# A pipelined image kernel on one core: the norm-to-scan chain moved into the last four units, and three units a direction summed by VectorE

## The chip, the core and the metric

The kernel runs on one core of one Trainium2 chip. A core has five engines that run their own instruction streams side by side: TensorE (PE, matrix products into PSUM), VectorE (DVE), ScalarE (ACT), GpSimd (POOL) and SyncE (SP, which here only issues DMAs). Each stream runs strictly in its written order; between the streams stand semaphores, so an instruction that waits holds up all that is written behind it on its engine. The metric is the time of one launch in microseconds (us).

## The reference, cut to what matters

For 16 images of 256 channels by 32 x 32 pixels, two residual blocks:

```python
x = x + L0(_gn(x))     # attention over pixels makes a 7x7 filter per image and channel; depthwise convolution
x = x + L1(_gn(x))     # selective scans at three resolutions, both directions, gated by silu(z)

def _ssm(x, ...):      # one scan: 128 channels, 16 states, L = 1024, 256 or 64 positions
    delta = softplus(dts @ dtw + dtb);  dA = exp(delta * A);  dBx = delta * B * x
    h = h * dA + dBx   # over the L positions, for each of 16 states
    y = sum over the 16 states of h * C,  + x * Dv;  then a layer norm over the channels
y3 = ssm(f3) + flipped ssm(f3);  y2 = the same of f2 + up2(y3);  y1 = the same of f1 + up2(y2)
out = conv1x1(y1 * silu(z))
```

f1 is a 1x1 projection of the normed image, f2 and f3 come from it by 2 x 2 convolutions of stride 2.

## The kernel before, in words

**Pipeline.** `stages` writes for each engine a loop over images. Its body works on three images at once: i is in its scans (L1), j in its depthwise convolution and then in its norm, projections and first chunks (the beginning of L1), m in the making of its filters (the beginning of L0). The body has 37 units, k = 0 to 36, and then a `bridge` that ends image i and starts the scans of j. So in the next body j is i. Bodies with all three images run 14 times; one before and two after the loop, and one at the very start, lack some.

**Units.** `UNITS` lists the scans: unit 0 is the third level (64 positions, 16 states at once, both directions), units 1 to 4 the second level (256 positions, 4 states each, both directions), units 5 to 20 the first level forward (1024 positions, one state each), units 21 to 36 the first level backward. A product q is one unit and one direction. For a first-level unit k:
- SP reads the rows B and C of that state, spread over all partitions, into `bb` (two buffers) and `cb` (three buffers) (`get_b`, `get_c`).
- POOL multiplies `bb` by `u` into `bx` (`inputs`, line 1315), one unit ahead.
- ACT makes the decays exp(delta*A) in PSUM, `slot_b`, one half of 512 positions at a time (`decay`, line 1173).
- DVE scans each half into PSUM, `slot_c` (`scan`, line 552), and multiplies it by C into SBUF, `h` (`weigh`, line 561). The second half of a unit is weighed within the next unit.
- POOL adds `h` to the running sum `y` (`gather`, line 1343), one unit behind. `h` has three buffers.

**The image in the convolution.** PE does the 7 x 7 depthwise filter as 98 taps of six matmuls each (`taps`, line 790) with diagonal matrices that ACT makes (`make_row`, line 1059, 14 a row of the filter, in portions `row_parts` of 3 and 4). The last taps are in unit 32. `BRIDGE_TAPS` says how many taps of the next image are put into the last units and the bridge, and `ROOM` spreads the rest over the units (`taps_at`). PREP is unit 33.

**The last four units and the bridge.** DVE adds the convolution to the image (`conv_add(j, 1)`, line 486) and takes its statistics (`b_s0`, line 431) at the end of unit 33. PE and ACT turn them into mean and root in units 34 and 35 (`sums1`, `sums2`, `gn_spread`, `b1`), ACT writes the normed image `xg` (line 1105) in unit 35, PE projects it to f1 in unit 36 (`project_f`), and ACT copies f1 (`copy_f(j, 0)`, line 1112) in unit 36. In the bridge follow f2 and f3 (`lower`), then the chunks 0 and 1, which make delta and the rows B, C of the third and second level: `chunk` on PE (lines 831, 832), `chunk_exp` on ACT (lines 1124 to 1133), `chunk_first` on DVE (line 500), `chunk_log` on ACT (1139), `chunk_last` on DVE (508, 510), `chunk_low` on POOL (1285, 1287). Between them stand the last two norms of image i (`norm_centre`, `norm_square`, `norm_spread`, `norm_root`, `norm`), its `output` into `ob`, and at the end on DVE `silu_clip` and the two scans of the third level (`scan_least`, line 525). On ACT the bridge ends with the decays of unit 1 (they wait for `output`, which shares PSUM with them), `y_start`, `keep_x`, 21 diagonals and `copy_x`; chunk 2 comes right behind, in unit 0. For the image m, ACT writes the padded fp16 copy (`prep`, line 1048) in unit 33 and DVE its lower half (`low_half`, line 444) in unit 34.

## Time and profile before

| | |
|---|---|
| median of 3 runs | 4224.79 us (4222.85 to 4224.82) |
| the profiled execution, its time | 4222.54 us |
| its span, first to last instruction | 4220.7 us |
| POOL busy | 3290.3 us (78%) |
| DVE busy | 3209.0 us (76%) |
| PE busy, weight loads beside it | 3109.9 us (74%), 1400.2 us (33%) |
| ACT busy | 2693.2 us (64%) |
| DMA engines, mean busy share | 46.4% |

How to read it: no engine is busy for more than four fifths of the span, so the time is made of stretches with different limits. One body of the loop, about 250 us, is repeated with hardly a difference, and is read below in one instance, from 1202.6 to 1454.2 us of the span. In the rows an idle time in brackets is that of the engine just before the instruction, with what ended it.

### The profile page before, as it was taken

The page shows a single profiled execution, that of the slowest core. Times are in us where ns is not written, and L with a number is a line of the kernel's source. Part 1 is how long each engine was busy: PE and PEld are TensorE (multiplying, and loading weights), DVE is VectorE, ACT ScalarE, POOL GpSimd, SP SyncE. Part 2 cuts the span into 40 slices and gives each one's busy share as a digit, 9 for nine tenths or more (in the row PEclk, how much of TensorE's full clock was granted, in tenths as well). Part 3 has the DMA queues.
Part 4 walks back from the last instruction along what each step waited for, and adds up shares of the span by engine and source line. Part 5 has one row for each costly group of instructions (what it writes and reads, how often), then busy time and mean ns, then how long its engine had stood idle before and what let it go on. Part 6 is the DMA issues. An engine that isn't in the chain of part 4 may idle for free.

```text
span 4220.7 us, 53011 instructions
## 1 busy us (share of the span) xinstructions
PE 3109.9 (74%) x12620; PEld 1400.2 (33%) x12620; DVE 3209.0 (76%) x3975; ACT 2693.2 (64%) x6662; POOL 3290.3 (78%) x1908
## 2 busy tenths in 40 slices
PE   6978777887777788777777877788787778877511
PEld 3433333333333333333333433333333333333200
DVE  1058788787877878787887878788787887878877
ACT  4467766666766666666656766665677666666532
POOL 0059698796968969697896969889696987969797
PEclk8989888998888899889898988999898889988755
DMA  1025455453545545354553544445354554635544
GB/s 41 1 101 195 147 163 169 157 205 127 186 150 166 186 136 204 134 178 152 170 201 122 199 149 165 161 168 203 119 195 145 167 170 157 204 118 192 163 165 167
DMA packets 187275, 664.08 MB, mean 157 GB/s; under 512 B 22736, under 2 KB 24672, under 8 KB 186976
## 3 DMA queue, kind: packets, MB, share of 16 engines
q1 hardware_dynamic: 186976, 661.47, 46.4%
q14 instruction: 280, 2.29, 0.2%
q8 instruction: 19, 0.31, 0.0%
HBM read 639.76 MB, written 21.63 MB: 157 GB/s over the span
## 4 chain that ended last, share of the span: by engine, by line
POOL 28%; issue 19%; ACT 16%; PE 14%; DVE 13%; DMA 7%; POOLq 1%; DVEq 1%; SPq 0%; ACTq 0%
POOL bx L1315 13%; POOL y L1343 7%; DMA bb<-bc_rows 7%; ACT diag L1059 7%; PE pconv L790 6%; POOL h L1338 5%; DVE h L561 4%; DVE slot_c L552 2%; POOL bx L1318 2%; DVE rs L508 2%; ACT slot_b L1173 2%; PE pm L832 1%; PE pm L807 1%; PE pm L831 1%; DVE rs L500 1%
## 5 line engine op out<-in xcount | busy, mean ns | idle before, releaser
L790 PE MATMUL pconv<-pad,diag 128*128 128x512 f16 x9408 | 2270.5, 398 | 314.3 <-ACT diag L1059 210.0
L790 PEld LDWEIGHTS pconv<-pad,diag 128*128 128x128 f16 x9408 | 932.0, 100 | 1618.0 <-issue 346.0
L1343 POOL TENSOR_TENSOR y<-y,h 128x1024 f32<-128x1024 f32 (+2 forms) x672 | 1324.5, 1971 | 162.9 <-DVE h L561 139.6
L1173 ACT ACTIVATE slot_b<-delta,nega 128x512 f32<-128x512 f32 (+1 forms) x1280 | 805.4, 639 | 951.3 <-DVE slot_c L552 911.6
L1315 POOL TENSOR_TENSOR bx<-bb,u 128x1024 f32<-128x1024 f32 x512 | 1220.1, 2383 | 31.9 <-DMA bb<-bc_rows 31.9
L552 DVE TENSOR_TENSOR_SCAN slot_c<-slot_b,bx 128x512 f32<-128x512 f32 (+1 forms) x1024 | 954.4, 956 | 315.6 <-POOL bx L1315 214.6
L561 DVE TENSOR_TENSOR h<-slot_c,cb 128x512 f32<-128x512 f32 x1280 | 860.6, 674 | 35.9 <-POOL y L1343 35.9
L552 DVE TENSOR_TENSOR_SCAN slot_c<-slot_b,slot_c,bx 128x512 f32<-128x512 f32 x512 | 663.6, 1296 | 74.5 <-ACT slot_b L1173 18.2
L1059 ACT ACTIVATE diag<-id,chi 128x128 f16<-128x128 f16 x1568 | 498.1, 387 | 10.3 <-PE pconv L790 9.6
L1059 ACT ACTIVATE diag<-id,clo 128x128 f16<-128x128 f16 x1568 | 496.4, 386 | 0.0
L1338 POOL TENSOR_TENSOR h<-h 128x512 f32<-128x512 f32 (+3 forms) x384 | 349.9, 911 | 20.9 <-DVE h L531 3.4
L1285 POOL TENSOR_TENSOR delta<-delta,rs 128x512 f32<-128x512 f32 (+1 forms) x96 | 97.7, 1017 | 324.6 <-DVE rs L510 324.6
L1318 POOL TENSOR_TENSOR bx<-bb,u 128x1024 f32<-128x1024 f32 x64 | 158.8, 2482 | 125.5 <-DMA bb<-bc_rows 97.9
L500 DVE SCALAR_TENSOR_TENSOR rs<-qs,es 128x512 f32<-128x512 f32 (+1 forms) x96 | 64.9, 676 | 223.6 <-ACT qs L1133 223.6
L831 PE MATMUL pm<-f,wbc 128*32 128x512 f32 (+1 forms) x192 | 102.3, 620 | 147.0 <-ACT delta L1129 74.2
L1295 POOL TENSOR_TENSOR f<-f,lnw 128x98 f32<-128x98 f32 x16 | 6.2, 388 | 182.8 <-ACT f L1003 182.8
L1139 ACT ACTIVATE qs<-qs 128x512 f32<-128x512 f32 (+1 forms) x96 | 50.5, 526 | 153.7 <-DVE rs L500 153.7
L852 PE MATMUL pm<-es,ones 128*128 128x512 f32 (+1 forms) x128 | 62.7, 573 | 113.2 <-ACT es L1183 113.2
L846 PE MATMUL pm<-y,cen 128*128 128x512 f32 (+1 forms) x128 | 60.3, 554 | 89.2 <-POOL y L1343 40.6
L722 PE MATMUL pm<-ident,xh 128*128 128x128 f32 x256 | 47.0, 343 | 98.3 <-ACT xg L1094 72.1
L832 PE MATMUL pm<-f,wdelta 128*128 128x512 f32 (+1 forms) x192 | 116.9, 698 | 0.0
L695 PE MATMUL pconv<-sg,grp 128*128 128x8 f32 x32 | 9.5, 371 | 145.5 <-DVE sg L431 145.5
(171 smaller groups left out, 3095.9 us busy)
## 6 DMA issues: line engine op xcount, KB each, us to landing
bb<-bc_rows SPq DMA_DIRECT2D x592, 512.0 KB, 4.4
cb<-bc_rows SPq DMA_DIRECT2D x592, 512.0 KB, 4.4
xr<-in_x SPq DMA_DIRECT2D x16, 1024.0 KB, 5.0
out<-ob SPq DMA_DIRECT2D x16, 1024.0 KB
bc_rows<-rows SPq DMA_DIRECT2D x64, 64.0 KB, 1.6
w<-in_w SPq DMA_DIRECT2D x2, 256.0 KB
wc<-in_wc SPq DMA_DIRECT2D x2, 256.0 KB
bc_rows<-rows SPq DMA_DIRECT2D x16, 32.0 KB, 4.0
```

The costliest lines, as they stand in the source:

```text
L500: nc.vector.scalar_tensor_tensor(er[:, k, 0:n], qs[:, k, 0:n], 1.0, es[:, k, 0:n], ALU.subtract, ALU.subtract).then_inc(ch_err.sem, 1)
L552: ins = nc.vector.tensor_tensor_scan(hv, av, bv, start, ALU.mult, ALU.add)
L561: nc.vector.tensor_tensor(half(h[:, q % HR], b), bank(slot_c, b), half(cb[:, k % CR], b), ALU.mult).then_inc(q_pr.sem, 1)
L790: ins = nc.tensor.matmul(bank(pconv, k), w, pad[:, t, part, rows:rows + 16, dx:dx + W], start=first and m == 0, stop=last and m == 2)
L831: nc.tensor.matmul(bank(pm, 0)[0:2 * NS, 0:n], wbc[:, st, :], f[:, fc:fc + n], start=True, stop=True).then_inc(ch_bc.sem, 1)
L832: nc.tensor.matmul(bank(pm, 1)[:, 0:n], wdelta[:, st, :], f[:, fc:fc + n], start=True, stop=True).then_inc(ch_dt.sem, 1)
L1059: ins = nc.scalar.activation(diag[:, r % RING, m, dx, :], id16[:, :], ACT.Copy, scale=(chi, clo)[m][:, t, dy * KK + dx:dy * KK + dx + 1])
L1173: ins = nc.scalar.activation(slot_b[:, o:o + w], delta[:, so + c:so + c + w], ACT.Exp, scale=nega[:, st, n0 + n:n0 + n + 1])
L1315: ins = pool.tensor_tensor(bx[:, k % 2, :], bb[:, k % BR, :], us, ALU.mult)
L1318: ins = pool.tensor_tensor(o, bb[:, k % BR, :].rearrange("p (m l) -> p m l", m=m), us[:, None, :].to_broadcast([P, m, ln]), ALU.mult)
L1338: pool.tensor_tensor(src[:, 0:m], src[:, 0:m], src[:, m:2 * m], ALU.add).then_inc(n_y.sem, 1)
L1343: pool.tensor_tensor(yv, yv, src[:, 0] if len(src.shape) == 3 else src, ALU.add).then_inc(q_y.sem, 1)
```

## The change

Two things are changed together.

**The chain moves.** In DVE's stream `conv_add(j, 1)` and `b_s0(j)` go from the end of unit 33 to its start. The sums on PE go from unit 34 to 33, `project_f` from 36 to 34, `lower` from the bridge to 35, `chunk(j, 0)` from the bridge to 36. In ACT's stream the spread, the root and the normed image go into unit 33, `copy_f` 0 and 1 into 35, `copy_f` 2, `chunk_exp(j, 0)` and `chunk_log(j, 0)` into 36, and `prep(m)` from the end of unit 33 to the end of unit 34. On DVE `chunk_first(j, 0)` stands ahead of the products of unit 36 and `chunk_last(j, 0)` behind them. In the bridge the first `scan_least` comes ahead of `norm(i, 4)` and the second behind `norm(i, 5)`; the 16 decays of the third level come ahead of `norm_square(i, 4)`. On PE unit 36 is `chunk(j, 0)` and three taps, and the bridge is `chunk(j, 1)`, one tap, `norm_centre` 4 and 5, one tap, `norm_spread` 4 and 5, two taps, `project_z`, `output`, three taps. SP issues `get_b(j, 0)` before it waits for the last products. `BRIDGE_TAPS` puts 11 taps ahead of unit 0 where there were 9.

**VectorE sums three units a direction.** `OWN` names the states 3, 8 and 13 of the first level: units 8, 13 and 18 forward, 24, 29 and 34 backward. POOL's `gather` leaves them out. DVE writes the first of each direction (units 8 and 24) straight from PSUM into `ob`, which is free then; for the others it multiplies within PSUM (`slot_c`) and then adds to `ob`, two instructions a half for one. The four norms of the first level add `ob` by a second matmul of 512 columns with `cen` (`norm_centre`).

```diff
+OWN = (3, 8, 13)
+def own(q):
+    u, _ = PRODUCTS[q]
+    return UNITS[u][0] == 1 and UNITS[u][3] in OWN
...
             def weigh(i, q, p):
...
+                if own(q):
+                    part, total = bank(slot_c, b), half(ob[:, PRODUCTS[q][1]], b)
+                    if UNITS[k][3] == OWN[0]:
+                        if p == 0:
+                            dve.wait_ge(ob_free.sem, ob_free.at(i + 1, 0))
+                        nc.vector.tensor_tensor(total, part, half(cb[:, k % CR], b), ALU.mult).then_inc(q_pr.sem, 1)
+                        return
+                    dve.wait_ge(q_h.sem, q_h.at(i, half_at(q, 1) + 1))
+                    nc.vector.tensor_tensor(part, part, half(cb[:, k % CR], b), ALU.mult).then_inc(q_own.sem, 1)
+                    dve.wait_ge(q_own.sem, q_own.at(i, 2 * kept(q) + p + 1))
+                    nc.vector.tensor_tensor(total, part, total, ALU.add).then_inc(q_pr.sem, 1)
+                    return
...
 @@ VectorE, bridge @@
                 if j is not None:
-                    chunk_first(j, 0)
-                if j is not None:
-                    chunk_last(j, 0)
+                    chunk_first(j, 1)
+                    scan_least(j, 0)
                 if i is not None:
                     norm(i, 4)
                 if j is not None:
-                    chunk_first(j, 1)
+                    chunk_last(j, 1)
                 if i is not None:
                     norm(i, 5)
                 if j is not None:
-                    chunk_last(j, 1)
+                    scan_least(j, 1)
                 if i is not None:
                     output(i, 0)
                     output(i, 1)
                 if j is not None:
                     silu_clip(j)
-                    scan_least(j, 0)
-                    scan_least(j, 1)
...
 @@ VectorE, unit @@
+                if j is not None and k == PREP:
+                    conv_add(j, 1)
+                    b_s0(j)
+                if j is not None and k == NU - 1:
+                    chunk_first(j, 0)
                 if i is not None:
                     products(i, k)
...
-                if k == PREP:
-                    if j is not None:
-                        conv_add(j, 1)
-                        b_s0(j)
                 if k == PREP + 1:
                     if m is not None:
                         low_half(m)
+                if j is not None and k == NU - 1:
+                    chunk_last(j, 0)
...
 @@ TensorE, norm_centre @@
+                last = max(v for v in range(NP) if own(v) and PRODUCTS[v][1] == d)
+                pe.wait_ge(q_pr.sem, q_pr.at(i, weighed(last)))
+                nc.tensor.matmul(o, cen[:, :], src, start=True, stop=False)
+                nc.tensor.matmul(o, cen[:, :], ob[:, d, c0:c0 + n], start=False, stop=True).then_inc(n_yc.sem, 1)
...
 @@ ScalarE, unit @@
+                if j is not None and k == PREP:
+                    row_parts(j, m, k, 0)
+                    act_b.start(act, j)
+                    gn_spread(act_b, j, sg, pconv, b_sums, b_spread)
+                if i is not None:
+                    if 1 <= k < NU - 1:
+                        decay(i, k + 1, 0)
+                if j is not None and k == PREP:
+                    b_root(j)
+                else:
+                    row_parts(j, m, k, 0)
+                if j is not None and k == PREP + 2:
+                    copy_f(j, 0)
                 if i is not None:
                     if 1 <= k < NU - 1:
                         decay(i, k + 1, 1)
+                if j is not None and k == PREP:
+                    b_normal(j)
+                if j is not None and k == PREP + 2:
+                    copy_f(j, 1)
                 if j is not None and k == PREP + 3:
-                    copy_f(j, 0)
+                    copy_f(j, 2)
+                    chunk_exp(j, 0)
                 row_parts(j, m, k, 1)
+                if j is not None and k == PREP + 3:
+                    chunk_log(j, 0)
...
-                    if k == PREP:
+                    if k == PREP + 1:
                         prep(m)
...
 @@ TensorE, unit @@
-                if m is not None and k == PREP + 2:
-                    taps(m, 0, BRIDGE_TAPS[1])
...
+                if j is not None and k == PREP + 1:
...
+                    project_f(j, 0)
+                    project_f(j, 1)
+                if k == PREP + 2:
+                    if j is not None:
+                        lower(j, 0)
+                    if m is not None:
+                        taps(m, 0, BRIDGE_TAPS[1])
+                    if j is not None:
+                        lower(j, 1)
                 if k == PREP + 3:
                     if j is not None:
...
+                        chunk(j, 0)
                     if m is not None:
                         taps(m, BRIDGE_TAPS[1], BRIDGE_TAPS[2])
...
-BRIDGE_TAPS = (0, 1, 3, 3, 3, 3, 6, 9)
+BRIDGE_TAPS = (0, 1, 4, 5, 6, 8, 11)
```

## Rows read from the trace of the kernel before

**Rows 1.** Stretch, length; busy PE, PEld, DVE, ACT, POOL (count); PE clock, DMA, GB/s

```profile
1202.60:1264.40 61.80, 42.20 (x136) 18.92 (x135) 42.69 (x49) 47.91 (x131) 29.09 (x16) 0.81 0.31 108
...
1277.10:1392.60 115.50, 87.92 (x350) 36.77 (x348) 95.75 (x121) 73.22 (x175) 106.88 (x65) 0.87 0.52 169
1392.60:1454.20 61.60, 56.19 (x281) 28.71 (x281) 52.46 (x65) 34.82 (x84) 61.52 (x31) 1.00 0.65 219
```

**Rows 2.** Waits between 1392.6 and 1454.2 us: total, times, longest, in us

```profile
DVE slot_c L552 <- POOL bx L1315: 4.5, 7, 0.8
...
PE pm L745 <- ACT f L1007: 2.2, 1, 2.2
```

**Rows 3.** Single lines over the span: count, duration in ns as min/median/max

```profile
L1343 POOL TENSOR_TENSOR y<-y,h x672: 317/2352/2815, 271.0 to 4197.7; 128x1024 f32<-128x1024 f32 x128, 128x256 f32<-128x256 f32 x32, 128x64 f32<-128x64 f32 x8
L444 DVE TENSOR_TENSOR pad<-xh,pad x32: 1223/1678/3366, 66.7 to 3711.8; 128x1024 f16<-128x1024 f32 x32
L561 DVE TENSOR_TENSOR h<-slot_c,cb x1280: 664/673/693, 270.4 to 4196.9; 128x512 f32<-128x512 f32 x183
```

**Rows 4.** Group by line: two operands, one in PSUM (busy us, mean ns | idle)

```profile
L619 DVE TENSOR_TENSOR o<-slot_b,sz 128x512 f32<-128x512 f32 x16 | 11.1, 692 | 0.6
```

**Rows 5.** Timeline of DVE, units 33 to 36 (start us, us, instruction, idle before)

```profile
1202.57 1.23 DVE L552 TENSOR_TENSOR_SCAN slot_c<-slot_b,bx 128x512 f32<-128x512 f32 x1
...
1206.30 0.69 DVE L603 TENSOR_TENSOR pm<-pm,rs 128x512 f32<-128x512 f32 x1
...
1208.77 1.28 DVE L486 SCALAR_TENSOR_TENSOR xn<-pconv,csc,xn 128x1024 f32<-128x1024 f32 x1
1210.09 2.47 DVE L431 BATCH_NORM_STATS2 sg<-xn 128x6 f32<-128x512 f32 x4
...
1216.19 4.96 DVE L444 TENSOR_TENSOR pad<-xh,pad 128x1024 f16<-128x1024 f32 x2
...
1229.96 1.27 DVE L561 TENSOR_TENSOR h<-slot_c,cb 128x512 f32<-128x512 f32 x2
```

**Rows 6.** Timeline of ACT, units 33 to 36 and chunk 0

```profile
1213.69 2.02 ACT L1048 ACTIVATE pad<-xh 128x1024 f16<-128x1024 f32 x2
...
1217.03 0.97 ACT L1059 ACTIVATE diag<-id,clo 128x128 f16<-128x128 f16 x3
...
1221.73 0.15 ACT L969 ACTIVATE sg<-pconv 128x4 f32<-128x4 f32 x1
...
1223.23 2.37 ACT L1105 ACTIVATE xg<-xn,sg 128x1024 f32<-128x1024 f32 x2
1225.51 0.67 ACT L1173 ACTIVATE slot_b<-delta,nega 128x512 f32<-128x512 f32 x1
...
1238.27 0.21 ACT L1124 ACTIVATE rows<-pm 32x64 f32<-32x64 f32 x1 [0.39 <-PE pm L831]
```

**Rows 7.** Timeline of DVE in the bridge and unit 1

```profile
1239.62 0.23 DVE L500 SCALAR_TENSOR_TENSOR rs<-qs,es 128x64 f32<-128x64 f32 x1 [8.39 <-ACT qs L1133]
...
1246.11 0.70 DVE L603 TENSOR_TENSOR slot_b<-slot_b,delta 128x512 f32<-128x512 f32 x1 [4.49 <-ACT delta L1196]
...
1255.02 1.61 DVE L628 SCALAR_TENSOR_TENSOR ob<-slot_c,vec,xc 128x512 f32<-128x512 f32 x2
...
1257.74 4.53 DVE L525 TENSOR_TENSOR_SCAN h<-a,b 128x1040 f32<-128x1040 f32 x2
```

**Rows 8.** Timeline of ACT, end of the bridge and chunk 2

```profile
1256.66 1.67 ACT L1173 ACTIVATE slot_b<-delta,nega 128x256 f32<-128x256 f32 x4 [2.73 <-DVE ob L628]
...
1271.18 0.57 ACT L1124 ACTIVATE rows<-pm 32x512 f32<-32x512 f32 x1
```

**Rows 9.** Timeline of PE: a centre matmul, the last taps, the bridge

```profile
1194.63 1.12 PE L846 MATMUL pm<-y,cen 128*128 128x512 f32 x2 [1.34 <-DVE o L588]
...
1200.36 2.83 PE L790 MATMUL pconv<-pad,diag 128*128 128x512 f16 x12
...
1238.43 1.89 PE L846 MATMUL slot_b<-y,cen 128*128 128x512 f32 x2
```

More of the change, by code:

```diff
@@ L87, in weighed, with added, kept @@
     return q + 1 if q < 2 else 2 * q
+OWN = (3, 8, 13)
+def own(q):
+    u, _ = PRODUCTS[q]
+    return UNITS[u][0] == 1 and UNITS[u][3] in OWN
+def added(q):
+    return sum(not own(v) for v in range(q))
+def kept(q):
+    return sum(own(v) and UNITS[PRODUCTS[v][0]][3] != OWN[0] for v in range(q))
 NHALF = 2 * (NP - 2)
@@ L863, in some @@
                         taps(m, BRIDGE_TAPS[lo], BRIDGE_TAPS[hi])
+                if j is not None:
+                    chunk(j, 1)
                 some(2, 3)
-                if j is not None:
-                    lower(j, 0)
-                some(3, 4)
-                if j is not None:
-                    lower(j, 1)
-                some(4, 5)
-                if j is not None:
-                    chunk(j, 0)
                 if i is not None:
@@ L875, in bridge @@
                     norm_centre(i, 5)
-                if j is not None:
-                    chunk(j, 1)
+                some(3, 4)
                 if i is not None:
@@ L880, in bridge @@
                     norm_spread(i, 5)
-                some(5, 6)
+                some(4, 5)
                 if j is not None:
@@ L1237, in unit @@
             def unit(i, j, m, k):
-                if j is not None and k == PREP + 1:
-                    act_b.start(act, j)
-                    gn_spread(act_b, j, sg, pconv, b_sums, b_spread)
-                if j is not None and k == PREP + 2:
-                    b1(j)
                 if i is not None:
```

56 lines of the change are left out of this document (25 added, 31 removed).

## The prediction

> **What bounds the kernel now.** I first read the busy time by stretches of one body, here 251.6 us long (1202.6 to 1454.2 us). From 1392.6 to 1454.2 us, the last first-level units ahead of unit 33, POOL is busy for 61.52 of 61.60 us: it sets the pace, and DVE idles for 61.60 - 52.46 = 9.1 us, half of it in waits for POOL's `bx` (4.5 us in 7 waits) [rows 1, 2]. PE is close behind: 56.19 us at the full clock. Here a product taken from POOL is worth something. From 1202.6 to 1264.4 us, units 33 to 36 and the bridge, it is the other way round: POOL is busy for 29.1 of 61.8 us, DVE for 42.7, ACT for 47.9, PE for 42.2 [rows 1]. Nothing is full, so this stretch is a chain over several engines. The timelines show it: on ACT diagonals stand between the links, unit by unit [rows 6]; DVE is idle for 8.39 us before `chunk_first(j, 0)` and 4.49 us before `norm(i, 4)` [rows 7]; and ACT, once `output` is done, works without a stop from 1256.66 to chunk 2 at 1271.18 us [rows 8]. Chunk 2 starts the next image's units, so what comes late at `output` comes late everywhere behind.
>
> **Part 1, the sums on VectorE.** POOL loses six additions of 2.35 us an image [rows 3]. DVE pays nothing for units 8 and 24 (one product a half, into `ob` and not `h`). For units 13, 18, 29 and 34 a half costs two instructions with one operand in PSUM, 0.69 us each [rows 4], for one of 0.67 [rows 3]: +0.71 a half, +1.4 a unit, 5.7 an image. A product within PSUM isn't in these rows; I take the nearest one. Its bounds: 0 more, or twice 0.69 a half if reading and writing PSUM don't overlap (+1.4 a unit again). What it brings depends on the place:
> - Units 18, 24 and 29 lie in or at the stretch that POOL bounds. It needs 3 x 2.35 = 7.05 us less there. DVE can give up its 9.1 us of idle time less 2 x 1.4, but part of that is the pipeline between instructions. PE has 61.6 - 56.2 = 5.4 us to give, less two further centre matmuls of 1.1 us each [rows 9], plus one tap less (6 of the 12 matmuls in 2.83 us, 1.4 us) [rows 9]: 4.6 us. I take -3.5 us a body; bounds 0 and -6.
> - Unit 8's saved time meets units in which DVE has no idle time, and unit 13 ends at chunk 4, which waits for `norm(i, 1)` on DVE. I take 0 and +0.7 us.
> - Unit 34 lies in the chain, below.
>
> **Part 2, the chain in the last units.** I lay the new streams out from the start of unit 33 on DVE, 1202.57 us, as zero, with the durations of before.
> - `conv_add` now stands first. The last taps end at 1203.19 [rows 9], 0.6, and norm 3's second centre matmul, ahead of them on PE, adds 1.1. So DVE waits until 1.7; 1.28 and 2.47 us [rows 5] bring the statistics to 5.5 (before: 1212.56, 10.0). The start is 4.5 us earlier, as meant.
> - DVE then does unit 33, 3.7 us (1202.57 to 1206.30), norm 3 with 2.4 (1206.30 to 1208.77) and unit 34, 3.7 and half of unit 34's extra, 0.7: it is done at 16.1.
> - ACT: sums, spread and their PE steps bring it to 8.1, root 1.5 (1221.73 to 1223.23), decay 0.6, `xg` 2.4 [rows 6], four diagonals 1.2: 13.8. Unit 34 has 14 diagonals and two decays; before, 1217.03 to 1221.73 held 14 and one, 4.7 us, so 5.3: 19.1. Only now comes `prep`, 2.0 us [rows 6]: 20.1 for its first half, 21.1 for the second.
> - `low_half` on DVE waits for it: **4 us of idle time that wasn't there**. Behind it on DVE are queued units 35 and 36, and for them wait POOL and ACT's decays. It runs while POOL has nothing to do, so its halves take 1.22 us, the minimum, and not 4.96 together [rows 3, 5]: done at 22.6.
> - ACT's `copy_f(j, 0)` stands behind the decay of unit 36, which needs unit 35's first scan, at 23.8. Before, from that decay (1225.51) to the end of `chunk_exp(j, 0)` (DVE goes on at 1239.62) it took 14.1 us with 28 diagonals [rows 6, 7]; now 20 stand there (-2.3) and the waits for `lower` are about as long: 12.1. So `chunk_exp(j, 0)` is done at 36.0. **The chain has moved by four units of program and by 1 us of time** (before 37.05).
> - But `chunk_first(j, 0)` now stands ahead of unit 36 on DVE, and DVE is done with unit 35 at 27.0 (22.6 + 3.7 + 0.7). It waits for **9 us**. Queued behind it: unit 36's scans and products, so POOL's last two sums, both centre matmuls, norms 4 and 5, `output`. Unit 36 takes 4.4 us (until 40.6) where it was done at 28.7 (1229.96 + 1.27).
> - From there: POOL's last sum until 43.0; two centres of four matmuls, 4.4 us at the rate of 1194.63, 7.2 at that of 1238.43 [rows 9], I take 4.4: 47.5; one tap and two spreads 51.0; root; norm 4 from 51.3, 2.2 us; `chunk_last(j, 1)` 0.9; norm 5 2.1: 56.4. `scan_least(j, 1)` has two SBUF operands and meets POOL's `bx` of unit 1: 2.3 us [rows 7] after a wait of 1.8: 60.5. `output` 3.2 us [rows 7]: 63.7. Before it ended at 1256.63, 54.1. So `output` comes **9.6 us later**; ACT's unbroken work from there to chunk 2 is the same [rows 8].
> - The two taps that leave units 0 to 32 for the bridge lie there beside waits; SP's earlier `get_b(j, 0)` ends nothing late.
>
> What I take for the shared path: the shortest `low_half` is 1.22 us, the longest 3.37 [rows 3]. The Trainium skill says in "SBUF — State Buffer", section "SBUF: two separate sides", that DVE with two SBUF inputs and GpSimd lock the shared port pair against each other for a whole instruction. By that rule the sums moved to DVE cost no lock, since one operand is in PSUM, and the trace agrees: 1280 products take 664 to 693 ns whatever POOL does [rows 3]. Without it `low_half` would end 2.5 us later and the scan 1.8 us earlier.
>
> **The sum.** A body: 9.6 + 0.7 - 3.5 = +6.8 us; 14 bodies, +95. The transition without m has no diagonals in the chain, so the waits are shorter: +3. The first pass, which has no scans to wait for but `prep` in the chain: +2. The last image alone: up to six sums of POOL less, against DVE's 5.7 and colder centres: -4. Together +96 on 4222.5, the profiled execution (which lies 2.3 below the median of 4224.8): 4319, on the median's scale **4321 us**.
>
> **The rivals.**
> 1. Slower by more: the centres and the taps at the lower clock (+2.8 a body), no gain in POOL's stretch (+3.5 against my sum). For it: the clock of the stretch is 0.81 already [rows 1], and PE will idle more. +12 a body, 4395 us.
> 2. Slower by less: POOL's relief in full (-6), the scan not held up (-1.8). +2.5 a body, 4260 us.
> 3. **Faster.** One mechanism: chunk 0's `qs` reaches DVE when it is done with unit 35. It decides at 27.0 in my count, 9 us ahead of 36.0; then `output` comes 0.6 us later and not 9.6, a body is 0.6 + 0.7 - 3.5 = -2.2, and the last image's 4 us less come on top: about 4190. For it: the 8.39 us that DVE idles there now [rows 7] would be filled by unit 36. Against it: ACT's order. The diagonals, the decay of unit 36 and `prep` stand ahead of `copy_f`, and ACT is busy for nearly all of it [rows 6].
> 4. No change: the wait is about 3 us long, and both parts cancel: +0 to +0.5 a body.
>
> **How the numbers follow.** Forecast 0.52, rival 1 0.16, rival 2 0.14, rival 3 0.13, rival 4 0.05. The range reaches from below rival 2 to a little above rival 1, 4245 to 4405; rivals 3 and 4 are left out, 0.18. 0.2% is 8.4 us, about what a measurement of this kernel can tell from no change. Faster 0.13, same 0.05, slower 0.82.
>
> **What would show it.** In the timeline of DVE: a wait of some 4 us before L444, of some 9 us before the first L500 with two units' products behind it, and none or little before norm 4. ACT's pads after 14 diagonals. The body longer by some 7 us, with POOL's busy time lower by 14 us and its idle time higher by 21. Between the middle of the backward units and unit 33 the pace of POOL's stretch a few us shorter. I am wrong if L500 for chunk 0 starts without a wait, if `output` ends less than 5 us later against unit 33's start, or if POOL's stretch shrinks by 7 us or more.

## The result, and the profile after

| kernel | median of the runs, us | profiled span, us | PE clock |
|---|---|---|---|
| before | 4223.8 (4221.4 to 4224.8) | 4220.7 | 0.873 |
| after | 4438.5 (4432.6 to 4441.0) | 4435.1 | 0.854 |

The ratio is 1.051, 95% interval 1.049 to 1.053: **slower, by 215 us**, where +96 was forecast and 4405 us was the range's upper end. Every time below is a median of runs in the chip's fast state; the one profiled run of e8 was in the slow state (7468 us), so e8 has a time and no stages.

Where the time went can be read off one event an image, the end of the last `output` step on VectorE (before L628, after L661). The first stands at 506.0 us before and at 530.3 us after (+24.3). Thirteen bodies follow, +183.8 (14.1 each, forecast 6.8), then the transition without m, +11.5 (forecast 3), and the last image, -5.2 (forecast -4). So most of the miss lies in the bodies, the rest in the first pass and the transition.

The means over the thirteen bodies, by stage, in us. A stage begins and ends at the start of a named instruction, `output` at its end; "late units" are first-level units 18 to 32:

| stage | before | after | change | forecast |
|---|---|---|---|---|
| `output` to chunk 2 | 17.6 | 17.6 | 0 | 0 |
| to unit 7 | 44.7 | 44.7 | 0 | 0 |
| unit 7 to unit 10 | 17.0 | 19.9 | **+2.9** | 0 |
| to chunk 5 | 31.3 | 30.3 | -1.0 | +0.7 |
| to unit 18 | 15.6 | 17.0 | +1.4 | 0 |
| late units | 70.7 | 71.8 | **+1.1** | -3.5 |
| unit 33, chain, bridge, to the end of `output` | 52.6 | 62.4 | **+9.8** | +9.6 |

The body of before that the prediction was read from (1202.6 to 1454.2 us) turns out to be the odd one of the thirteen. In it the centre matmuls of norms 4 and 5 took 1.89 and 1.91 us, in the next body and the others 1.08 and 1.02, and its last stage took 54.1 us where the other twelve took 52.4:

```profile
1490.09 1.08 PE L846 MATMUL slot_b<-y,cen 128*128 128x512 f32 x2
1491.00 1.02 PE L846 MATMUL slot_c<-y,cen 128*128 128x512 f32 x2
```

**The bridge.** The timeline of VectorE after, units 33 to the bridge (start us, us, instruction, idle before it), which answers to [rows 5, 7]:

```profile
1260.80 1.28 DVE L507 SCALAR_TENSOR_TENSOR xn<-pconv,csc,xn 128x1024 f32<-128x1024 f32 x1 [0.70 <-PE pconv L823]
1262.12 2.47 DVE L452 BATCH_NORM_STATS2 sg<-xn 128x6 f32<-128x512 f32 x4
...
1279.17 2.36 DVE L465 TENSOR_TENSOR pad<-xh,pad 128x1024 f16<-128x1024 f32 x2 [3.62 <-ACT pad L1086]
...
1296.92 0.23 DVE L521 SCALAR_TENSOR_TENSOR rs<-qs,es 128x64 f32<-128x64 f32 x1 [10.94 <-ACT qs L1173]
...
1301.78 2.43 DVE L531 TENSOR_TENSOR rs<-rs,es 128x64 f32<-128x64 f32 x1
1304.13 0.41 DVE L521 SCALAR_TENSOR_TENSOR rs<-qs,es 128x256 f32<-128x256 f32 x1
1308.82 2.33 DVE L546 TENSOR_TENSOR_SCAN h<-a,b 128x1040 f32<-128x1040 f32 x1 [4.28 <-ACT a L1204]
1312.07 0.70 DVE L636 TENSOR_TENSOR slot_b<-slot_b,delta 128x512 f32<-128x512 f32 x1 [0.93 <-ACT delta L1236]
...
1320.66 1.40 DVE L661 SCALAR_TENSOR_TENSOR ob<-slot_c,vec,xc 128x512 f32<-128x512 f32 x2
```

Counted from 1260.1, where unit 32 ends: the statistics are done at 4.5, `low_half` waits 3.6 us, chunk 0's first step comes at 36.8 after a wait of 10.9, norm 4 at 52.0, `output` ends at 62.0. The forecast had 5.5, 4, 36.0 after 9, 51.3 and 63.7.

ScalarE and TensorE between them show why the chain doesn't arrive earlier although it starts earlier (columns as above; answers to [rows 6, 9]):

```profile
1270.71 5.49 PE L831 MATMUL pm<-xg,wf 128*128 128x512 f32 x8 [3.42 <-ACT xg L1145]
1286.24 3.78 PE L849 MATMUL pm<-f,wc 128*128 128x256 f32 x8 [10.04 <-ACT f L1152]
```

```profile
1278.08 2.02 ACT L1086 ACTIVATE pad<-xh 128x1024 f16<-128x1024 f32 x2
1282.71 0.69 ACT L1213 ACTIVATE slot_b<-delta,nega 128x512 f32<-128x512 f32 x1 [2.61 <-DVE slot_c L573]
1283.34 0.97 ACT L1097 ACTIVATE diag<-id,clo 128x128 f16<-128x128 f16 x3
1284.21 0.97 ACT L1097 ACTIVATE diag<-id,chi 128x128 f16<-128x128 f16 x3
1285.09 1.09 ACT L1152 ACTIVATE f<-pm,bf 128x1024 f32<-128x1024 f32 x1
1286.09 0.67 ACT L1213 ACTIVATE slot_b<-delta,nega 128x512 f32<-128x512 f32 x1
1290.05 0.47 ACT L1152 ACTIVATE f<-pm,vec 128x256 f32<-128x256 f32 x1 [3.29 <-PE pm L849]
```

The projection `f` is in PSUM at 1276.2. ScalarE copies it at 1285.1, 8.9 us later: ahead of it in its queue stand four diagonals, `pad`, a decay (L1213) that waits 2.61 us for VectorE's scan of unit 35, and six more diagonals; and that scan stood behind `low_half`, which waited for `pad`.

**Unit 7.** What TensorE has in its unit 5 runs while VectorE is at unit 7. TensorE after, in its unit 5, then ScalarE at the same place, then TensorE before at the same place:

```profile
1383.62 5.78 PE L823 MATMUL pconv<-pad,diag 128*128 128x512 f16 x18 [15.77 <-ACT diag L1097]
1389.23 0.28 PE L728 MATMUL pm<-sa,grp 128*128 128x8 f32 x2
```

```profile
1389.55 0.17 ACT L996 ACTIVATE sa<-pm 128x4 f32<-128x4 f32 x1 [2.79 <-PE pm L728]
```

```profile
1318.18 2.74 PE L790 MATMUL pconv<-pad,diag 128*128 128x512 f16 x6 [13.64 <-ACT diag L1059]
1320.71 0.43 PE L695 MATMUL pm<-sa,grp 128*128 128x8 f32 x2
```

`BRIDGE_TAPS` now ends at 11 and not 9, so `taps_at` rounds the remaining taps differently: three taps (18 matmuls) instead of one (6) stand ahead of the key chain's sums, and ScalarE, which has the next decays behind them, waits 2.79 us. The diff's last line, a list for the last units and the bridge, moved what stands in unit 5.

**The late units.** The fifteen units 18 to 32, before and after: stretch, length; busy PE, PEld, DVE, ACT, POOL; clock, DMA, GB/s:

```profile
1383.50:1454.20 70.70, 64.86 (x312) 32.98 (x313) 60.46 (x74) 42.54 (x101) 70.62 (x34) 0.96 0.65 218
```

```profile
1450.80:1523.90 73.10, 66.27 (x307) 33.89 (x306) 66.59 (x78) 39.96 (x92) 64.76 (x31) 0.93 0.61 213
```

POOL lost 5.9 us of work (7.05 in the forecast) and no longer fills the stage. DVE gained 6.1; it and TensorE (66.59 and 66.27 us) are now the busiest. Only 2.8 of DVE's 6.1 are the four extra instructions of units 18 and 29. The rest are two small steps that were short before. The lines of the weights' maximum and of the 49x49 diagonal, before and after (ns min/median/max):

```profile
L477 DVE TENSOR_SCALAR wsc<-sa x16: 168/526/535, 60.9 to 3672.4; 128x2 f32<-128x2 f32 x16
L454 DVE TENSOR_SCALAR dg<-ident,sk x16: 241/647/657, 37.1 to 3634.5; 49x49 f32<-49x49 f32 x16
```

```profile
L498 DVE TENSOR_SCALAR wsc<-sa x16: 169/2124/2133, 58.4 to 3866.9; 128x2 f32<-128x2 f32 x16
L475 DVE TENSOR_SCALAR dg<-ident,sk x16: 241/2108/2239, 36.3 to 3832.6; 49x49 f32<-49x49 f32 x16
```

The same instruction over two elements a partition takes 0.17 us alone and 2.12 us here. Who holds it up shows beside GpSimd:

```profile
1497.65 2.36 POOL L1389 TENSOR_TENSOR y<-y,h 128x1024 f32<-128x1024 f32 x1
```

```profile
1497.92 2.12 DVE L498 TENSOR_SCALAR wsc<-sa 128x2 f32<-128x2 f32 x1
```

It starts 0.27 us after a POOL sum and ends with it (1500.01 and 1500.04). Before, VectorE reached this step near the end of a POOL instruction, 0.5 us before it was over; now it hits the beginning of one. In every run the step lasts as long as POOL's instruction still has to go: 0.68 us left and 0.70 long once in e6, 1.95 left and 1.98 long in e2, 2.1 left and 2.13 long after.

The body shown is one of two kinds, and the mean of +1.1 hides both. In eight of the thirteen bodies the 49x49 step is held up too (2.10 to 2.24 us), VectorE then waits 3.3 to 3.6 us for TensorE's product for `fi` (L771), and the stage takes 73.0 to 73.3 us. In the other five the step takes 0.24 us, the wait is 1.8 to 1.9 us, and the stage takes 69.6 to 69.8, 1.0 **less** than before. What parts them is less than half a microsecond: in the eight the step begins 0.15 to 0.28 us behind the start of a POOL product (`bx`), in four of the five 0.06 to 0.14 us ahead of one, in the fifth none is near. One of the five:

```profile
1190.30:1260.10 69.80, 66.08 (x314) 33.45 (x314) 64.67 (x78) 39.94 (x92) 64.74 (x31) 0.96 0.65 223
```

### The profile page after: what moved, and what is told of

The parts are those of the page before. It is cut to its first block, busy times and chain, and to the rows that moved or that the text cites. A ratio compares the mean times of both kernels' runs of the same rounds, so it can differ in the third digit from the quotient of the medians.

```text
span 4435.1 us, 53179 instructions
## 1 busy us (share of the span) xinstructions
PE 3265.9 (74%) x12748; PEld 1475.6 (33%) x12748; DVE 3345.0 (75%) x4103; ACT 2700.2 (61%) x6662; POOL 3060.2 (69%) x1812
## 4 chain that ended last, share of the span: by engine, by line
DVE 23%; issue 20%; POOL 19%; PE 17%; ACT 17%; DMA 1%; DVEq 1%; POOLq 1%; SPq 0%; ACTq 0%
PE pconv L823 8%; POOL bx L1359 8%; ACT diag L1097 6%; DVE h L594 5%; POOL h L1384 5%; DVE slot_c L573 4%; POOL y L1389 3%; POOL bx L1362 2%; DVE rs L529 2%; DVE rs L531 2%; ACT slot_b L1213 1%; PE pm L849 1%; DVE rs L521 1%; PE pm L771 1%; DVE slot_c L588 1%
## 5 line engine op out<-in xcount | busy, mean ns | idle before, releaser
L823 PE MATMUL pconv<-pad,diag 128*128 128x512 f16 x9408 | 2313.2, 403 | 323.6 <-ACT diag L1097 244.9
L823 PEld LDWEIGHTS pconv<-pad,diag 128*128 128x128 f16 x9408 | 943.8, 102 | 1652.6 <-issue 338.9
L1389 POOL TENSOR_TENSOR y<-y,h 128x1024 f32<-128x1024 f32 (+2 forms) x576 | 1099.1, 1908 | 552.3 <-DVE h L594 529.5
L1213 ACT ACTIVATE slot_b<-delta,nega 128x512 f32<-128x512 f32 (+1 forms) x1280 | 806.1, 640 | 1031.1 <-DVE slot_c L573 972.5
L1359 POOL TENSOR_TENSOR bx<-bb,u 128x1024 f32<-128x1024 f32 x512 | 1205.5, 2356 | 109.3 <-DMA bb<-bc_rows 88.4
L594 DVE TENSOR_TENSOR h<-slot_c,cb 128x512 f32<-128x512 f32 x1088 | 732.1, 674 | 62.9 <-POOL y L1389 62.9
L1097 ACT ACTIVATE diag<-id,chi 128x128 f16<-128x128 f16 x1568 | 498.1, 387 | 11.5 <-PE pconv L823 10.9
L1384 POOL TENSOR_TENSOR h<-h 128x512 f32<-128x512 f32 (+3 forms) x384 | 348.1, 906 | 17.6
L521 DVE SCALAR_TENSOR_TENSOR rs<-qs,es 128x512 f32<-128x512 f32 (+1 forms) x96 | 82.0, 854 | 252.1 <-ACT qs L1173 250.3
L1362 POOL TENSOR_TENSOR bx<-bb,u 128x1024 f32<-128x1024 f32 x64 | 156.6, 2448 | 144.5 <-DMA bb<-bc_rows 115.9
L849 PE MATMUL pm<-f,wc 128*128 128x256 f32 (+1 forms) x256 | 74.9, 451 | 142.6 <-ACT f L1152 142.6
L831 PE MATMUL pm<-xg,wf 128*128 128x512 f32 x128 | 93.5, 898 | 55.3 <-DVE o L621 31.8
L546 DVE TENSOR_TENSOR_SCAN h<-a,b 128x1040 f32<-128x1040 f32 x32 | 78.2, 2444 | 63.4 <-ACT a L1204 63.4
```

Source lines behind the costliest of these rows:

```text
L521: nc.vector.scalar_tensor_tensor(er[:, k, 0:n], qs[:, k, 0:n], 1.0, es[:, k, 0:n], ALU.subtract, ALU.subtract).then_inc(ch_err.sem, 1)
L594: nc.vector.tensor_tensor(half(h[:, q % HR], b), bank(slot_c, b), half(cb[:, k % CR], b), ALU.mult).then_inc(q_pr.sem, 1)
L823: ins = nc.tensor.matmul(bank(pconv, k), w, pad[:, t, part, rows:rows + 16, dx:dx + W], start=first and m == 0, stop=last and m == 2)
L849: ins = nc.tensor.matmul(pm[:, o:o + n], w[:, m, :], src[:, :, m // 2, :, m % 2], start=(m == 0), stop=(m == 3))
L1097: ins = nc.scalar.activation(diag[:, r % RING, m, dx, :], id16[:, :], ACT.Copy, scale=(chi, clo)[m][:, t, dy * KK + dx:dy * KK + dx + 1])
L1213: ins = nc.scalar.activation(slot_b[:, o:o + w], delta[:, so + c:so + c + w], ACT.Exp, scale=nega[:, st, n0 + n:n0 + n + 1])
```

## Experiments

All were timed beside before (4222 to 4225 us on the same chip). Diffs are against the kernel named.

**e1: the chain without the own units** (against after).

```
-OWN = (3, 8, 13)
+OWN = ()
```

> The chain and BRIDGE_TAPS as changed, but POOL adds up all units and DVE none (no second centre matmul). Theory A (the loss is the chain's): of the 14.0 us that a body became longer, 9.6 lie between chunk 0's first step on DVE and the end of output, 2.9 ahead of unit 7 and 2.5 in the late first-level units. The first two stay here, less 2.2 us for the two further centre matmuls of norms 4 and 5 and less the 2.5: a body of 249.4 + 9.3 - 2.2 + 2.9 = 259.4 us, about 4370 us in all. Rival B (the loss is the sums' on DVE): a body within 4 us of before, at most 4285 us.

4401.2 us (4399.5 to 4404.4), ratio 1.042 [1.040, 1.044]. The own units are 37 us of the 215; the chain's part, with the tap list of e4 in it, is 178. B falls. A's 4370 was 31 us too low. One reason is in the stages: without the second centre chunk 0 to the end of `output` should have been 2.2 us shorter, and it took 25.9 us, where after has 25.2. In the changed kernel the second centre costs nothing there.

**e2: the own units without the chain** (against before: `own`, `added`, `kept`, the own branch of the product, the second centre matmul).

> The chain as before, but DVE sums units 8, 13, 18, 24, 29 and 34 as in the change. By the prediction's part 1: +0.7 at unit 13, -3.5 in the late units, +2 for the two centre matmuls of norms 4 and 5, +0.7 for unit 34: about 0, 4215 to 4230 us. Theory A2 (what the trace of the changed kernel showed in the late units, +2.5 there instead of -3.5, comes with the sums alone): a body 5 to 6 us longer, about 4305 us. Rival C (the sums are a gain by themselves, the trouble in the late units came with the moved chain): 4180 us or less.

4281.8 us (4279.7 to 4290.4), ratio 1.015 [1.013, 1.016]: +59, where the prediction's part 1 gives about 0 and A2 4305. **The half of the change that should bring 3.5 us a body in the late units costs 3.9 over the body.** By stages: late units +1.6, chunk 0 to the end of `output` +1.6, the rest +0.7. The late units take 69.0 to 75.3 us, and again the longest are bodies in which the 49x49 step was held up (7 of 13).

**e3: chunk 0's steps on VectorE behind unit 36** (against after).

```
-                if j is not None and k == NU - 1:
-                    chunk_first(j, 0)
                 if i is not None:
                     products(i, k)
...
                 if j is not None and k == NU - 1:
+                    chunk_first(j, 0)
                     chunk_last(j, 0)
```

> The changed kernel with one edit: on DVE chunk_first(j, 0) stands behind the products of unit 36 again, ahead of chunk_last(j, 0). Theory A: the wait of 10.9 us goes, unit 36's products, POOL's last sums and the centre matmuls come up to 11 us earlier, and then chunk 0 itself or ACT's order ends last in the bridge: 6 to 9 us a body less, 4300 to 4350 us. Rival D (DVE was waiting there for something that ends late anyway, the 16 decays and the norms wait for chunk 0 all the same): at most 2 us a body less, 4410 us or more.

4410.5 us (4404.4 to 4417.8): only 28 less; D is right. The wait of 10.9 us with unit 36 queued behind it is real and nearly free: POOL's last sum starts 29.6 us behind `conv_add(j, 1)` (1287.6 less 1258.0) and not 41.0 (1301.8 less 1260.8), and yet `output` ends only 1.8 us earlier a body.

**e4: the tap schedule of before** (against after; the list is what `taps_at` gave before, with 11 for its first entry).

```
-    return BRIDGE_TAPS[-1] + -(-(TAPS - BRIDGE_TAPS[-1]) * sum(ROOM[:n]) // sum(ROOM[:PREP]))
+    return TAPS_AT[min(n, PREP)]
```

> The changed kernel with one edit: the taps are spread over units 1 to 32 exactly as before (one tap in unit 5 behind the row of diagonals that PE waits for, not three); only unit 0 has the two fewer. Theory E: the 2.9 us ahead of unit 7 (PE's three slow taps stand ahead of the sums that ACT waits for, and ACT's decays behind them) go: a body 261.0 us, about 4400 us. Rival F: the stretch is bound by POOL again, and the time stays within 5 us of 4438.

4405.7 us (4392.4 to 4417.3): 33 less, as E says, with a spread of 25 us. Units 7 to 10 are back at 16.9 us; of the 2.9 us a body, 1.5 come back later (in the profiled run, the slowest of the four).

**e5: norms 4 and 5 first on ScalarE and VectorE** (against e3, in the bridge; ScalarE's, then VectorE's calls, conditions left out).

```
                     chunk_exp(j, 1)
-                    decay(j, 0, 0)
-                    chunk_log(j, 1)
...
                     norm_root(i, 5)
+                    decay(j, 0, 0)
+                    chunk_log(j, 1)
...
                     chunk_first(j, 1)
-                    scan_least(j, 0)
                     norm(i, 4)
-                    chunk_last(j, 1)
                     norm(i, 5)
-                    scan_least(j, 1)
+                    chunk_last(j, 1)
...
                     silu_clip(j)
+                    scan_least(j, 0)
+                    scan_least(j, 1)
```

> The kernel of e3 (chunk 0's VectorE steps behind unit 36) with one further edit: in the bridge ScalarE does norms 4 and 5 (squares and roots) ahead of the third level's 16 decays and of chunk 1's logarithm, and VectorE does both norms ahead of chunk 1's last step and puts the third level's two scans at the bridge's end. TensorE's order is untouched. Theory G, ScalarE's and VectorE's orders gate the image's end: the 3.9 us of decays and the 3.1 us of chunk and scan go from between the norms, 3 us a body or more, 4410 - 42 = about 4365 or below. Theory H, TensorE's order gates it: in the trace of e3 TensorE ends centre 5 at 1302.5, spreads at 1306.1, and the outputs start at 1311.9 only because 12 tap matmuls and z (1305.9 to 1312.1) stand ahead of them, so almost nothing: 4395 to 4415.

4408.9 us (4403.8 to 4411.4), 2 us from e3. H is right: two of the bridge's three queues put in order bring nothing while the third isn't.

**e6: TensorE's bridge too** (against e5, conditions left out; ScalarE's squares come ahead of `chunk_exp(j, 1)` as well).

```
-                taps(m, BRIDGE_TAPS[1], BRIDGE_TAPS[2])
-                chunk(j, 1)
                 norm_centre(i, 4)
                 norm_centre(i, 5)
+                chunk(j, 1)
+                taps(m, BRIDGE_TAPS[1], BRIDGE_TAPS[1] + 1)
                 norm_spread(i, 4)
                 norm_spread(i, 5)
-                project_z(j)
+                taps(m, BRIDGE_TAPS[1] + 1, BRIDGE_TAPS[2] + 1)
                 output(i, 0)
+                taps(m, BRIDGE_TAPS[2] + 1, BRIDGE_TAPS[2] + 2)
                 output(i, 1)
+                project_z(j)
+                taps(m, BRIDGE_TAPS[2] + 2, BRIDGE_TAPS[6])
```

> The kernel of e5 with TensorE's order turned too: behind chunk 0 the two centres, then chunk 1, 6 tap matmuls, the spreads, 18 tap matmuls, output of half 0, 6 tap matmuls, output of half 1, then z and the last taps; ScalarE's squares come ahead of chunk 1's exponentials. No work is added or taken away. Theory H: in the trace of e3 the sums of unit 36 are there at 1290.0 and TensorE is free for the centres at 1292.5, not 1298.9; the outputs leave TensorE at about 1308.5 and not at 1315.5, 7 us a body, 14 x 7 = 98: about 4310, or 4350 if half of it is given back behind the bridge. Theory I, the time is not at the image's end: the decays, scans and taps that now come later take the place of what is saved, 4390 or above.

4367.8 us (4362.3 to 4375.4): -41. The stage to `output` shrinks by 5.8 us a body, where H says 7, but the next one, to chunk 2, grows from 18.1 to 21.2: half is given back behind the bridge, because z is now late.

**e7: e6 without own units, with the taps of e4.**

> The kernel of e6 without the own units (no unit is multiplied or summed out of PSUM by VectorE, all go to GpSimd as before) and with the tap schedule of e4. If the three parts add up: e6's time less the 37 us that the own units cost in e1 and less the 33 us that the tap rounding costs in e4: 70 below e6, so about 4240 if e6 gives 4310. If the chain's move has a cost besides these and the bridge's order, it is the distance from this time to the kernel before (4222.6).

4275.5 us (4274.0 to 4277.8): -92, 22 more than the parts' sum.

**e8: own units alone without the second centre** (against e2).

```
-                nc.tensor.matmul(o, cen[:, :], src, start=True, stop=False)
-                nc.tensor.matmul(o, cen[:, :], ob[:, d, c0:c0 + n], start=False, stop=True).then_inc(n_yc.sem, 1)
+                nc.tensor.matmul(o, cen[:, :], src, start=True, stop=True).then_inc(n_yc.sem, 1)
```

> The kernel of e2 (before with the own units alone) without the second centre matmul of norms 4 and 5: what stands in ob is not added, so the output lacks the three own units' part. Theory J, the second centre lies on the image's end: 2 pairs x 1.02 us from their rows, x 14 = 25 to 29 us, 4282 - 27 = about 4255. Theory K, the own units' cost lies in the late first-level units (VectorE's extra instructions and small steps behind GpSimd's bx, 2.8 us a body by the stages) and the centre's wait is covered: 4275 to 4282.

4244.3 us (4240.7 to 4260.9): 37 less than e2. K falls, and J's 4255 is 11 us above the measured time: in this kernel second centres lie on the path. The edit takes them out of all four norms of the first level and not only, as the text above has it, out of norms 4 and 5. The two pairs of norms 4 and 5 (1.02 us each) are 29 of the 37; the other 8 can be norms 2 and 3 or the spread of 20 us.

**e9: z behind the spreads** (against e7): `project_z(j)`, both outputs, then all of the bridge's taps.

> The kernel of e7 with one edit in TensorE's bridge: z's projection and both outputs directly behind the spreads, all tap matmuls of the bridge behind them. Theory H again: what e6 and e7 gave back lies behind the bridge (from the end of the output to chunk 2: 20.9 us in e7, 17.6 before the change), because z ends at 1274.4 and VectorE waits 3.7 us for ScalarE's copy of it. With z 8 us earlier this wait goes: 3.3 us a body, 14 x 3.3 = 46: about 4230. Rival: the taps pushed behind the outputs are late for the rows of the next image and take it back: 4265 to 4280.

4221.2 us (4218.4 to 4223.7), ratio 1.000 [0.999, 1.001]: -54. The chain's move with the queues in order costs nothing, and **brings nothing**. The wait it leaves, VectorE in e7 and TensorE in e9:

```profile
1256.58 0.22 DVE L521 SCALAR_TENSOR_TENSOR rs<-qs,es 128x64 f32<-128x64 f32 x1 [6.84 <-ACT qs L1176]
```

```profile
1228.94 3.36 PE L846 MATMUL pm<-f,wc 128*128 128x256 f32 x7 [8.81 <-ACT f L1150]
```

**e10: `prep` and the copy of f ahead of unit 34's last diagonals** (against e9, ScalarE alone).

```
-                if j is not None and k == PREP + 2:
-                    copy_f(j, 0)
...
+                if k == PREP + 1:
+                    if m is not None:
+                        prep(m)
+                    if j is not None:
+                        copy_f(j, 0)
                 row_parts(j, m, k, 1)
...
-                    if k == PREP + 1:
-                        prep(m)
```

> The kernel of e9 with one more edit, on ScalarE alone: the preparation of the image after next (pad's first half) and the copy of the first-level projection f go into unit 34, ahead of that unit's last diagonal writes, where e7 has the preparation behind these and the copy in unit 35 behind a decay. Theory L, the chain gains nothing from starting three units earlier because its first copy stands in ScalarE's queue behind decays that wait for VectorE: in the trace of e7 TensorE ends the projection at 1237.3, ScalarE copies it at 1245.1, and VectorE has nothing to do from 1249.8 to 1256.6; with the copy at about 1238 chunk 0's first step comes at about 1250, and pad comes 2.3 us earlier: 5.5 to 7 us a body, 14 x 6 = 84: about 4145, faster than the kernel before. Rival M, something else ends last by then (TensorE's bridge, GpSimd's sums of unit 36): at most 2 us a body, 4200 to 4230.

**4170.9 us** (4170.0 to 4172.2), ratio 0.988 [0.986, 0.990]. The mechanism is L's; the stage to chunk 0 is 5.7 us shorter:

```profile
1210.26 2.01 PE L846 MATMUL pm<-f,wc 128*128 128x256 f32 x8 [1.70 <-ACT f L1150]
```

```profile
1222.38 0.23 DVE L521 SCALAR_TENSOR_TENSOR rs<-qs,es 128x64 f32<-128x64 f32 x1 [2.85 <-ACT qs L1171]
```

But the time fell by 50 and not 84 us: of the 5.7 us a body 2.0 come back before the end of `output`, 0.6 elsewhere. The centre matmuls hold most of the 2.0. From the first to the last of norms 4 and 5 they take 2.1 us in e9 and 3.7 in e10 (means). The first pair, e7 and e10:

```profile
1255.39 1.08 PE L879 MATMUL slot_b<-y,cen 128*128 128x512 f32 x2
```

```profile
1222.09 2.07 PE L879 MATMUL slot_b<-y,cen 128*128 128x512 f32 x2 [0.73 <-POOL y L1389]
```

The granted clock was 1.00 (2.4 GHz) there in e7 and 0.50 (1.2 GHz) in e10. The 19.7 us before the centres and the time of the centres, e7 and then e10 (stretch, length; busy by engine; clock):

```profile
1235.70:1255.40 19.70, 8.18 (x30) 4.96 (x28) 10.25 (x11) 13.40 (x37) 8.87 (x4) 0.72 0.00 1
1255.40:1258.20 2.80, 2.80 (x10) 1.13 (x10) 0.22 (x1) 2.62 (x11) 0.00 (x0) 1.00 0.13 21
```

```profile
1202.30:1222.00 19.70, 11.72 (x34) 6.00 (x34) 14.64 (x15) 18.78 (x52) 12.14 (x6) 0.76 0.07 30
1222.00:1226.00 4.00, 3.91 (x5) 1.35 (x6) 0.68 (x3) 3.37 (x13) 0.47 (x3) 0.50 0.56 187
```

TensorE was not idle for longer in e10, but for less (busy 11.72 us against 8.18). What differs is where the low clock falls. In e7 one wait of 8.96 us stands ahead of `lower`, which then runs at 1.2 GHz (3.78 us); the centres come after the clock is back. In e10 `lower` runs at 2.4 GHz (2.01 us), waits of 2.47 and 3.18 us follow it, and the low clock meets the centres.

**e11: the same edit in the kernel after.**

> The kernel after with the same edit on ScalarE and nothing else (own units, tap schedule, chunk 0 ahead of unit 36 and the bridge's orders as in the change). Theory L: VectorE's wait for chunk 0 of 10.9 us at 1296.9 (ahead of unit 36 there) shrinks by 6 to 8 us, and it stands on the path: 4438 - 14 x 7 = about 4340. Rival M: 4410 or above.

4353.8 us (4348.5 to 4356.4): -85, chunk 0 comes 6.1 us earlier a body. So ScalarE's queue order by itself is 85 of the 215 us. About 0.7 us of the 6.2 us that a body is shorter are in the late units, where the 49x49 step was held up in 5 bodies and not in 8.

**e12: chunk 1's last step ahead of the norms** (against e10; the same move on ScalarE for its logarithm).

```
                     chunk_first(j, 1)
+                    chunk_last(j, 1)
                 norm(i, 4)
                 norm(i, 5)
-                    chunk_last(j, 1)
```

> The kernel of e10 with chunk 1's logarithm (ScalarE) ahead of the roots of norms 4 and 5 and chunk 1's last step (VectorE) ahead of both norms. In the trace of e10 GpSimd's products for unit 0 and 1 run at 1242.1 and 1247.8, under VectorE's two scans of the third level, and these take 6.65 us where they take 4.53 us in the trace of before, the products behind them 4.44 us in place of 2.33. Theory N, GpSimd's work holds these VectorE instructions up: with chunk 1's step 6 us earlier (VectorE has nothing to do for 1.6 us there) GpSimd's first product lies in front of the scans; 2 to 4 us a body, 4171 - 28 to 56 = 4115 to 4143. Rival, the next wait (GpSimd's second product waits for its DMA, or ScalarE's copy of x) is the bound and nothing comes of it: 4165 to 4175.

**4125.7 us** (4124.1 to 4130.3), ratio **0.977 [0.975, 0.979]**: the fastest here. VectorE's scans in e10 and e12:

```profile
1241.71 6.65 DVE L546 TENSOR_TENSOR_SCAN h<-a,b 128x1040 f32<-128x1040 f32 x2
1248.28 4.44 DVE L552 TENSOR_TENSOR h<-cb,h 128x1024 f32<-128x1024 f32 x2
```

```profile
1229.41 4.53 DVE L546 TENSOR_TENSOR_SCAN h<-a,b 128x1040 f32<-128x1040 f32 x2
1233.86 2.34 DVE L552 TENSOR_TENSOR h<-cb,h 128x1024 f32<-128x1024 f32 x2
```

The stage to chunk 2 is 1.2 us shorter, the one to `output` 1.6 (chunk 1's step no longer stands between norm 5 and `output`), the others 0.9 together: theory N and more.

**e13: the own units put back into e10.**

> The kernel of e10 with the own units of the change put back in. Theory A, they cost in this kernel what they cost alone: e2 less before, 57 us, gives 4171 + 57 = 4228. Theory C, they were priced in the wrong surroundings and pay once the chain no longer sets the end of the bridge: below 4171. Between them, 37 us as the distance of after to e1: 4208.

4254.0 us (4250.8 to 4259.2): +83, worse than alone (+59) and than A's 57. C falls. Of the 6.0 us a body, 2.3 are in the late units, where the 49x49 step is held up in 11 of 13 bodies, and 2.8 between chunk 0 and the end of `output`: here the two further pairs of centre matmuls come at the lower clock. All four pairs take 6.1 us (3.7 in e2), the two of e10 3.7. The first two of them:

```profile
1246.03 2.07 PE L880 MATMUL slot_b<-y,cen 128*128 128x512 f32 x2 [1.16 <-POOL y L1386]
1247.89 1.92 PE L881 MATMUL slot_b<-ob,cen 128*128 128x512 f32 x2
```

**e14: the own units without sums** (against e2).

```
-OWN = (3, 8, 13)
+OWN = (3,)
```

> Before with the own units cut to the two that need no sum (8 and 24, product straight into ob; four of e2's six, with an extra add for each half, stay as before); the second centre matmul stays. Of e2's 57 us the second centre is 27 (e8: 31). If the rest is the extra VectorE instructions of units 13, 18, 29 and 34, this gives before plus the centre: 4222 + 29 = about 4251. If the rest hangs on GpSimd's changed phase and not on VectorE's adds, 4265 to 4280.

4216.9 us (4215.7 to 4223.0), ratio 0.998 [0.997, 0.999]: 65 less than e2 and 7 less than before, below both expectations, which left out the two sums that POOL loses (e8's distance is 37 us and not the 31 quoted there). Its late units, and those of e2:

```profile
1380.30:1450.00 69.70, 66.69 (x316) 33.78 (x317) 62.05 (x74) 42.91 (x101) 68.41 (x33) 0.96 0.63 223
```

```profile
1401.00:1476.20 75.20, 71.09 (x316) 36.60 (x317) 66.46 (x78) 42.73 (x101) 64.69 (x31) 0.89 0.59 207
```

In e14 (first row) POOL is still the bound (68.41 of 69.70 us) and the stage 1.0 us shorter than before in all thirteen bodies, though the 128x2 step takes 2.13 us there too (median). So this step is held up whoever sets the pace; its place against POOL's instructions decides, and its 1.6 us more didn't keep the stage from being shorter. The 49x49 step isn't held up longer than before here (0.65 us). In e2 (second row, one of its longest bodies) VectorE has 66.46 us of work and TensorE 71.09 at a clock of 0.89, and the mean stage is 1.6 us longer than before. So two sums that POOL drops pay 1.0 us there, and four more that VectorE takes over cost more than they free. How much of that cost is VectorE's instructions and how much the waits for TensorE behind the 49x49 step, no run takes apart. The second centre is in e14 too and costs 1.6 us a body there (chunk 0 to `output`, 17.1 against 15.5).

## Why the prediction was right and wrong

**The chain, right in its steps, and with some luck in its sum.** Step by step within 2 us, and its sum +9.6 against +9.8: the wait ahead of `low_half` (4, measured 3.6), "moved by four units of program and by 1 us of time" (36.0, measured 36.8; before 37.05), the wait for chunk 0 (9, measured 10.9), `output`. Smaller terms stand against each other: POOL's `y` held up chunk 0's last step (L531, 2.43 us for 0.22), which the sum had not, and `lower` and the taps in the bridge ran at the lower clock (L849 3.78 us; 2.01 in e10), while the conv's statistics came 1 us sooner than forecast. The luck is in the two ends of the difference: the forecast's end of `output`, 63.7, is 1.3 us above the mean of 62.4, and the end that it was held against, 54.1, is 1.5 us above the mean of 52.6, because it came from the odd body.

**Its cause, half right.** The prediction called "`chunk_first` stands ahead of unit 36" the reason why `output` is late. e3 shows that this is worth 28 us of 178. Beside it stood two further queues that gate as much, TensorE's (18 tap matmuls and chunk 1 ahead of the centres, z ahead of the outputs) and ScalarE's; rival 3, priced at 4190 for chunk 0 coming earlier, would have needed those too. The text against rival 3, that ScalarE's diagonals, decay and `prep` stand ahead of `copy_f`, was the right place: e11 gives it 85 us.

**POOL's stretch, wrong in sign: -3.5 forecast, +1.1 measured, outside the bounds of 0 and -6.** The step that failed is "DVE can give up its 9.1 us of idle time less 2 x 1.4". It priced the extra instructions at 2.8 us, which they are (0.69 us each, as forecast; `ob<-slot_c,ob` took 690 to 693 ns), but not that VectorE's two small steps would meet POOL's instructions at another place: up to 3.1 us more (median 0.53 to 2.12 and 0.65 to 2.11), and behind the second of them a wait of 3.3 us or more for TensorE. Where only the first was held up, five bodies of thirteen, the stage came out at -1.0, inside the bounds but far from -3.5; where both were, at +2.4. The Trainium skill says in "SBUF — State Buffer", section "SBUF: two separate sides", that a VectorE instruction in a 2-port performance mode takes the same exclusive lock. The end of L498 with POOL's instruction agrees with such a lock; in which mode the step runs, no run shows. I had drawn on that section for two-input instructions alone. And the idle time of an engine that waits for another isn't a reserve to its last microsecond: of the 73.1 us after, VectorE is busy for 66.6 and TensorE for 66.3, and VectorE's waits for POOL are gone from the list of the longest.

**BRIDGE_TAPS, wrong: 0 forecast, 33 us measured (e4).** The step "the two taps lie there beside waits" looked at where the taps go and not at what their number does to the rounding of all the others. The cost was in TensorE's unit 5 (VectorE's units 7 to 9), 2.9 us a body.

**The second centre.** The centres of norms 4 and 5 took 4.4 us in the forecast and 3.7 in the trace (1304.26 to 1307.95). With the chain as before second centres are on the path (e8, 37 us for all four norms; 1.6 us a body for norms 4 and 5 in e14); in the changed kernel those of norms 4 and 5 aren't (e1). What norms 2 and 3 pay was not measured apart.

**The edges.** +10 us in the first pass beyond its body (forecast 2) and +11.5 in the transition without m (forecast 3) were estimates without a sum; no experiment took them apart, so they stay open. The last image is right (-5.2 against -4).

In the sum, a body: 9.8 + 2.9 + 0.4 + 1.1 = 14.2 us against 9.6 + 0 + 0.7 - 3.5 = 6.8. Of the miss of 118 us, the bodies are 7.3 x 14 = 102 and the edges 16. Rival 1 comes nearest, and its own terms (6.8 + 2.8 + 3.5) give 13.1 a body and not the 12 it was priced at. Its second term, no gain in POOL's stretch, came true. Its first didn't: in the timeline after, the centres run at the full clock (1.02 to 1.12 us a pair).

## What to carry to other kernels

When a chain over several engines is moved earlier, its gain is decided by the queue with the worst order: follow each link to the instruction that stands ahead of it on its engine, and ask whether that one waits for the engine that the chain was to relieve. Here the same move is worth +178 us, 0 or -98 us (e1, e9, e12), by the order of some ten calls in three queues (and, in the last two, the tap list of before).

An engine that is paced by another has less room than its idle time says: its own fill, and instructions that are short only because of the place, against the other's instructions, at which they fall. Take work off the bound without adding to the next one (e14, -7 us), rather than move it (e2, +59).

A body that is read for a forecast should be held against its neighbours: the one read here was the odd one of thirteen, and stages that look like one number (+1.1) can be two (-1.0 and +2.4).

A constant that feeds a schedule's rounding is a change to the whole schedule: compare the schedule's list entry by entry before pricing it.

## What the runs showed of the hardware

Not only instructions with two SBUF operands are held up by GpSimd: a TENSOR_SCALAR of VectorE over 128x2 f32 in SBUF took 2.12 us under a POOL TENSOR_TENSOR and 0.17 us alone, and one over 49x49 2.11 against 0.24. The first ended each time with POOL's instruction (0.50, 0.68, 1.95 or 2.1 us left when it began; 0.53, 0.70, 1.98 or 2.13 us long), while 128 sums of a PSUM and an SBUF operand stayed within 690 to 693 ns.

Making a chain shorter can move TensorE's low clock onto a dearer place. With the chain 5.7 us shorter (e10) `lower` ran at 2.4 GHz and not 1.2 (2.01 us for 3.78), and the centre matmuls behind it at 1.2 and not 2.4 (2.07 us for two in place of 1.08), though TensorE had been busy for more of the 19.7 us before them (11.72 against 8.18).
